# Summing neighbouring exponentials on GpSimd in layer 0's attention, ahead of the matmuls with ones

## The reference

```
scores = einsum('bhqd,bhkd->bhqk', Q, K) + mask      # causal, 1024 x 1024
attn = softmax(scores, axis=-1)
o = einsum('bhqk,bhkd->bhqd', attn, V)
return x + gelu(o) @ Wf + bf
```

## Time and profile before

| | |
|---|---|
| median of 3 runs | 2742.35 us (2739.61 to 2743.72) |
| profiled execution, its own time | 2725.8 us |
| its span | 2723.9 us |
| mean granted TensorE clock | 0.826 of 2.4 GHz |
| busy: TensorE, VectorE, ScalarE, GpSimd | 2218.2, 1513.9, 1402.7, 692.7 us |
| layer 0's attention, from its first matmul with ones to its last | 119 to 288, 779 to 941, 1429 to 1597, 2084 to 2252 us |

### The profile page before, as it was taken

One profiled execution on the slowest core, in us unless ns is written; L12 is line 12 of the kernel. 1 busy time (PEld: TensorE's weight loads), 2 busy tenths in 40 slices (PEclk: granted clock), 3 DMA queues, 4 the chain that ended last, 5 costly groups with the idle time before them and its releaser, 6 DMA issues. The chain is left out here.

```text
span 2723.9 us, 30057 instructions
## 1 busy us (share of the span) xinstructions
PE 2218.2 (81%) x10649; PEld 843.0 (31%) x10649; DVE 1513.9 (56%) x3298; ACT 1402.7 (51%) x2019; POOL 692.7 (25%) x717
## 2 busy tenths in 40 slices
PE   3799867778999886678998987767899998676789
PEld 1223332223433242222443233122343224222244
DVE  2554356666565255675655625577655544566642
ACT  1145437894234533898324453589522454378932
POOL 1012212332422211233331121133242121123324
PEclk9599876568999986676899988567799998666789
DMA  5200131001500023100430003210051002300012
GB/s 137 60 19 2 56 94 38 18 1 40 149 28 19 1 78 94 34 1 1 122 89 24 2 28 95 57 27 1 12 153 44 19 1 78 78 32 18 1 43 89
DMA packets 67845, 128.31 MB, mean 47 GB/s; under 512 B 11396, under 2 KB 24836, under 8 KB 63076
## 3 DMA queue, kind: packets, MB, share of 16 engines
q1 hardware_dynamic: 67696, 126.40, 17.0%
HBM read 109.99 MB, written 15.20 MB: 46 GB/s over the span
## 5 line engine op out<-in xcount | busy, mean ns | idle before, releaser
L1289 DVE TENSOR_REDUCE mx<-ps 128x1 f32<-128x512 f32 (+3 forms) x1248 | 640.0, 553 | 471.3 <-PE ps L655 360.3
L1057 ACT ACTIVATE pr<-ps 128x1024 f32<-128x1024 f32 (+3 forms) x672 | 516.3, 805 | 447.1 <-PE ps L725 444.5
L652 PE MATMUL ps<-kop,qop 72*128 72x512 bf16 (+6 forms) x1248 | 446.2, 380 | 146.0 <-DVE mx L1289 109.0
L725 PE MATMUL ps<-qop,kop 75*128 75x512 bf16 (+7 forms) x1344 | 416.0, 376 | 92.4 <-DVE wb L1349 34.7
L771 PE MATMUL ps<-pr,vt 128*32 128x512 f32 (+3 forms) x2688 | 355.2, 607 | 7.3 <-POOL pr L1576 6.3
L1576 POOL TENSOR_SCALAR_AFFINE_SELECT pr<-pr 128x512 f32<-128x512 f32 x224 | 150.3, 671 | 802.0 <-ACT pr L1057 800.9
L1114 ACT ACTIVATE pr<-ps 128x512 f32<-128x512 f32 x224 | 133.8, 598 | 344.0 <-PE ps L878 280.3
L652 PEld LDWEIGHTS ps<-kop,qop 72*128 72x128 bf16 (+1 forms) x1248 | 123.8, 102 | 544.6 <-DVE mx L1289 335.4
L725 PEld LDWEIGHTS ps<-qop,kop 75*128 75x128 bf16 (+1 forms) x1344 | 122.6, 105 | 325.3 <-ACT pr L1057 133.2
L888 PE MATMUL ps<-pr,w_down 128*128 128x512 f32 x384 | 197.8, 600 | 3.2 <-POOL pr L1567 3.2
L655 PE MATMUL ps<-maskqk,identb 128*128 128x128 bf16 x832 | 199.5, 247 | 0.0
(11 more groups left out here) (309 smaller groups left out, 2989.6 us busy)
## 6 DMA issues: line engine op xcount, KB each, us to landing
wb<-gates_scratch SPq DMA_DIRECT2D x192, 256.0 KB, 3.3
kop<-kparts_scratch SPq DMA_DIRECT2D x32, 576.0 KB
qop<-qparts_scratch SPq DMA_DIRECT2D x96, 192.0 KB
on<-hmax_scratch SPq DMA_DIRECT2D x8, 1024.0 KB, 5.3
kparts_scratch<-on SPq DMA_DIRECT2D x12, 256.0 KB, 2.9
qparts_scratch<-on SPq DMA_DIRECT2D x12, 256.0 KB, 4.5
qparts_scratch<-wb SPq DMA_DIRECT2D x12, 256.0 KB, 2.9
kparts_scratch<-wb SPq DMA_DIRECT2D x12, 256.0 KB, 4.5
```

What stands on the lines that cost most here:

```text
L652: mm = pe.matmul(o, qop[0:k, slot(l, u), j, qb * P:(qb + 1) * P], kop[0:k, slot(l, u), j, k0:k0 + wd], start=True, stop=not diag)
L725: mm = pe.matmul(o, kop[0:k, slot(l, u), 2 * pair + j, kb * P:(kb + 1) * P], qop[0:k, slot(l, u), 2 * pair + j, q0:q0 + wd], start=True, s ...
L1057: nc.scalar.activation(pr[:, g % 3, 2 * pair:2 * pair + 2, o0:o0 + wd], ps[:, bank:bank + 2, o0:o0 + wd], ACT.Exp).then_inc(a.exps, 1)
L1289: ins_ = nc.vector.tensor_reduce(mx[:, nth(l, u) % 2, j, qb, col % 2:col % 2 + 1], ps[:, bank, 0:wd], AX.X, ALU.max, negate=True)
```

## The change

Only layer 0 is touched. Full steps (s = 4 to 7) no longer run the quad with ones. GpSimd adds the exponentials of steps 4 and 5, then those of 6 and 7 (four heads by 512 columns each), into one buffer `pair_sum`, and TensorE runs one quad with ones over each sum: the first behind the value quad of step 7, the second behind step 9. A sum may be overwritten once its quad is done (`pair_used`). The exponentials of layer 0 get a fourth buffer, so that an exponential waits for the step four before it, and in addition for the sum that reads that buffer. The wait for the read-out of bank 5, which stood at step 4, moves to the first quad over a sum.

```diff
+def summed(s):
+    return 4 <= s < 8
+def pairs_until(g):
+    u, s = divmod(g, NS)
+    return 2 * u + (s - 4) // 2 + 1
...
+        depth = (4, 3)
+        def exp_slot(l, g):
+            return pr[:, g % 3] if l else (pr[:, 0], pr[:, 1], pr[:, 2], wb[:, 0])[g % 4]
+        pair_sum = wb[:, 1]
...
                         else:
                             pe.wait_ge(a.o_out, out_before(u, c))
-                            if l == 0:
-                                pe.wait_ge(a.s_out, NC * u + c)
+                            if l == 0 and c == 0:
+                                pe.wait_ge(a.s_out, NC * u)
...
-                        if l and j == 3:
+                        if j == 3 and (l or summed(s)):
                             mm.then_inc(a.pv, 1)
-                    if l == 0:
+                    if l == 0 and not summed(s):
...
+                    if l == 0 and s in (7, 9):
+                        pe.wait_ge(pair_ready, 2 * u + (s == 9) + 1)
+                        if s == 7:
+                            pe.wait_ge(a.s_out, NC * u + 1)
+                        for j in range(4):
+                            mm = pe.matmul(ps[32 * j:32 * j + 32, 5, :], ones32[:], pair_sum[:, j, :],
+                                           start=s == 7, stop=False, tile_position=(0, 32 * j))
+                        mm.then_inc(pair_used, 1)
...
-                        if g >= 3:
-                            act.wait_ge(a.pv, g - 2)
-                        nc.scalar.activation(pr[:, g % 3, 2 * pair:2 * pair + 2, o0:o0 + wd],
+                        if g >= depth[l]:
+                            act.wait_ge(a.pv, g - depth[l] + 1)
+                            if l == 0 and summed((g - depth[l]) % NS):
+                                act.wait_ge(pair_ready, pairs_until(g - depth[l]))
+                        nc.scalar.activation(exp_slot(l, g)[:, 2 * pair:2 * pair + 2, o0:o0 + wd],
...
             for g in range(UNITS * NS):
                 cut(0, g)
+                if g % NS in (5, 7):
+                    pool.wait_ge(at[0].exps, 2 * (g + 1))
+                    if pairs_until(g) > 1:
+                        pool.wait_ge(pair_used, pairs_until(g) - 1)
+                    nc.gpsimd.tensor_tensor(pair_sum, exp_slot(0, g - 1), exp_slot(0, g), ALU.add).then_inc(pair_ready, 1)
                 if g % NS == 4:
                     scale_out(g // NS, 0)
```

More of the change, by code:

```diff
@@ L511, in adaln_kernel @@
         v_ones, tables = sem("v_ones"), sem("tables")
+        pair_ready, pair_used = sem("pair_ready"), sem("pair_used")
         gb_in = [sem(f"gb_in{r}") for r in range(4)]
@@ L771, in values @@
                         mm = pe.matmul(ps[32 * j:32 * j + 32, 4, o0:o0 + wd], vt[:, kb, 32 * h:32 * h + 32],
-                                       pr[:, g % 3, j, o0:o0 + wd], start=kb == 0, stop=last,
+                                       exp_slot(l, g)[:, j, o0:o0 + wd], start=kb == 0, stop=last,
                                        tile_position=(0, 32 * j))
-                        if l and j == 3:
+                        if j == 3 and (l or summed(s)):
                             mm.then_inc(a.pv, 1)
-                    if l == 0:
+                    if l == 0 and not summed(s):
                         for j in range(4):
                             mm = pe.matmul(ps[32 * j:32 * j + 32, 5, o0:o0 + wd], ones32[:],
-                                           pr[:, g % 3, j, o0:o0 + wd], start=kb == 0, stop=last,
+                                           exp_slot(l, g)[:, j, o0:o0 + wd], start=s == 0, stop=last,
                                            tile_position=(0, 32 * j))
                         mm.then_inc(a.pv, 1)
+                    if l == 0 and s in (7, 9):
[6 more added lines that the diff above has]
+                        mm.then_inc(pair_used, 1)
                 def hyp_values(k):
@@ L1573, in cut @@
                 if diag:
-                    past = pr[:, g % 3, :, q0 - c * CH:q0 - c * CH + P]
+                    past = exp_slot(l, g)[:, :, q0 - c * CH:q0 - c * CH + P]
                     pool.wait_ge(at[l].exps, 2 * (g + 1))
```

## The result

Slower. The median of four runs is 2789.52 us (2776.95 to 2795.03) against 2740.98 us (2738.44 to 2743.72) for the kernel before, a ratio of 1.017 [1.0134, 1.0207]. The forecast was 2774 us, in a range of 2748 to 2808. The loss is 48.5 us where 32 were predicted. The profiled execution after took 2776.95 us (span 2775.2), the shortest of its four.

The account below looks back on a forecast made before the run. TensorE, busy 2218 of 2724 us with its full clock granted only part of the time, was taken as the bound. The terms -4.8 + 15.8 + 20.8 gave +32 us on 2742.35, so 2774 us, range 2748 to 2808.

Parts of the forecast that it names:

- The removed quads: Steps 4, 5 and 6 of units with pieces: each loses one quad, 3 x 0.88 = 2.64 us gained.
- The length of the addition: GpSimd addition of 2048 columns: 4.5 us, from the line through its product at 512 and 1024 columns.
- the upper end of 8.0: Longest addition considered, in us: four times the slowest GpSimd group of that size, 1.99 us in layer 1.
- The second addition and the cut behind it: GpSimd before step 8: addition waits for step 7's quads, then the cut; step 8's values at 904.5, 2.0 us lost again.
- units with pieces: Layer 0, 12 units of 44.8 us with VectorE busy 26.4: -0.4 us each before the clock.
- Step 9 and the DMA: End of units with pieces: second sum's quad adds 0.88 us; waits of 0.19 and 0.41 us for the maxima go.
- the term of -4.8 us: Units with pieces, clock left out: -0.4 us per unit, times 12.
- Units without pieces: Each batch's last unit, 4 in all, 26.0 us: +3.9 us each from the late second addition, +15.8 us in sum.
- The clock behind the stall: TensorE's quads behind the stall before step 8 run at half clock: 1.3 us in each of 16 units, +20.8 us.
- The fourth buffer: Layer 0's exponentials: values of three steps before were done anyway, by TensorE's order, so 0.
- the thinner steps: Steps 4 to 6: fall to half clock more often, but have one quad less to run slowly; taken to cancel.

Follow-up runs that it names:

- second profile: Both kernels run again unchanged, each with a new profile: 2739.49 us for the kernel before, 2780.25 us for the changed kernel.
- experiment 2: Changed kernel with a buffer of its own for the second sum, added in two instructions of 1024 columns: 2732.90 us, 0.9964 of the kernel before.
- experiment 4: Changed kernel adding only heads 0 and 1, whose sums stand in for heads 2 and 3: 2733.41 us, 0.9965 of the kernel before.
- experiment 5: Changed kernel with GpSimd's cut of step 8 put ahead of the second addition: 2736.17 us, 0.9997 of the kernel before.
- experiment 6: Changed kernel with the first sum's quad at step 6 in place of step 7: 2741.42 us, 1.0019 of the kernel before.
- Experiment 3: Changed kernel with filler matmuls on TensorE in the stall ahead of step 8's values: 2769.18 us, 1.0089 of the kernel before.
- experiment 7: Kernel before with only the fourth buffer for layer 0's exponentials, no sums: 2737.43 us, 1.0007 of the kernel before.
- experiment 10: Changed kernel without additions or quads over sums, full steps left out of the softmax's sums (measurement only): 2690.52 us, 0.9816 of the kernel before.
- experiment 8: Experiment 2 with the sums only in units with pieces, unit 3 as in the kernel before: 2711.40 us, 0.9882 of the kernel before.
- experiment 9: Experiment 8 with four small zero-weight matmuls ahead of each piece between values of steps 0 and 1: 2736.52 us, 0.9983 of the kernel before.

## Why the prediction was right, and what was mis-sized

The direction and the mechanism were right, and 2789.5 lies in the range. Point by point:

- *The removed quads* ("a quad less shortens such a step by its full 0.88 us"): 0.86 us in each of steps 4, 5 and 6. Right.
- *The length of the addition*, 4.5 us, which no row had: 4.50 and 4.52. Right; the upper end of 8.0 fell. The slow group of the earlier trace rows said nothing of this stage; the stage's own product at 1.283 us did. The GPSIMD Engine Reference of the Trainium skill (section 3.1, Elementwise) has 4497 ns for it, and the trace agrees with 4499.
- *The second addition and the cut behind it*: steps 7 to 8 take 7.26 us, forecast 7.22 (904.5 - 897.28). Right. (From the quad's end to the addition's start it is 0.18 us, 916.84 to 917.02, where the sum had 0.07.) Experiments 2, 4, 5 and 6 each take one link of that chain away (the buffer, the length, the order, the time of the quad), and each time the 5.24 us, or the same sum over two steps, are back in units with pieces.
- *Step 9 and the DMA*: +0.86 for the quad, and steps 10 to 11 go from 2.47 to 1.97 us. Right in kind, but the term of -4.8 us was too small. It took the 0.41 us of one unit for all twelve; four others waited 0.95 to 1.78. The twelve waits for the maxima's DMA were 9.0 us in all (second profile 9.6), and 0.7 (1.0) after, so 8.3 and 8.6 us were gained.
- *Units without pieces*: +3.9 us forecast without the clock (four of them are 15.6, where the sum has 15.8). Measured 30.94 against 25.29, +5.65, of which steps 8 to 9 (4.05 against 2.40) are the clock's: +4.0 without them.
- *The clock behind the stall*, 16 x 1.3 = 20.8 us. Steps 8 to 9 take 4.18 us in the mean with pieces (2.81 at full clock) and 4.13 without (2.40): 12 x 1.37 + 4 x 1.73, with 1.0 more in steps 9 to 10 of two units, make 24.4. Experiment 3 shows it to be the clock. It was between the cases that the trace had shown, and came out at the upper of them: nearly always one step's quads in full. The page TensorE: Matmul & The Clock Gate of the Trainium skill (The HAM clock gate) has an idle array fall to 1.2 GHz; here it fell behind an idle time of 1.95 us, with the clock at 0.53 in the window behind it.
- *The fourth buffer* at 0: 1.0007 in experiment 7. Right.

Two profiles of each kernel give this account, in us (each after against the before beside it):

```
                                         forecast  1st pair   2nd pair
12 units with pieces, layer 0              +10.8     +10.8      +15.3
4 units without pieces, layer 0            +21.0     +23.0      +21.9
layer 1's attention (no edit there)          0       +13.4       +3.4
everything else                              0        +4.0       +8.2
profiled execution                         +32       +51.2      +48.8
```

**The step that failed** is the one on the thinner steps: "I let these cancel". In the first profile of the kernel before six of the steps 5 to 6 and 6 to 7 are slow, in five units, 9.7 us in all with a little of steps 4 to 5; in the second four are, 6.6 us. After, none is. In their place the beginnings of units are slow: steps 1 to 2 over 3.7 us in 6 of 8 units 1 and 2 (7 in the second profile), where it was 1. Over all twelve units steps 0 to 3 take 8.3 us more in the first pair and 12.9 in the second. So it did nearly cancel in the first pair, but not because thin steps "have one quad less to run slowly", and that was luck; experiment 10 shows that those steps don't get slow more often for being thin. Of the 12.9 us, 5.2 are one unit, the first of batch 3; it begins just as slowly in experiment 7, which has the work of the kernel before, so it takes no change for that.

**What was mis-sized** is mainly the rest of the kernel, for which the sum had no term. Layer 0's attention accounts for 33.7 and 37.2 us, against 31.8 forecast; within it, in the first pair, the gain at the DMA was put too small by 3.5 us and the clock's price by 3.6, and the two cancel. 12 to 18 us lie outside it, where both kernels issue the same instructions. Of these, the 13.4 in layer 1 are an accident of the first profile of the kernel before: its four attentions took 1136.3 us there, but 1143.2 to 1152.3 in each of the twelve other profiles, of kernels from 0.98 to 1.017 alike. That accident doesn't explain the miss, though: the second pair ran within 0.5 us of the medians of the result, and has 37.2 us in layer 0's attention, 3.4 in layer 1's and 8.2 elsewhere. The last two, 11.6 us, aren't traced to a cause. Everything outside layer 0's attention took 2062.9 and 2074.5 us in the two profiles of the kernel before, 2071.1 in experiment 7, 2080.5 and 2086.9 after the change, and 2086.2 in experiment 4, which is faster than the kernel before. So the scatter between profiles is as large as what is to be explained; whether the change adds to it stays open.

## What to carry to other kernels

Before work is moved to a slower engine, look at what is queued behind it there, in order, and who waits for that: 4.5 us on an engine that was three quarters idle cost 48 us in all, and putting a 0.64 us instruction ahead of it gave the loss back. A sum that is to be overlapped needs a buffer of its own as well as an idle engine, and here it paid to leave it out where the steps are shorter than it is (experiment 8: both, 0.988). And price a stall of TensorE with the quads behind it at half clock: here 2 us of stall cost 3.4.

## What the runs showed of the hardware

- A GpSimd addition of float32 takes 2.34 us for 1024 columns and 4.50 to 4.52 for 2048, as its product does for 512 and 1024: a line with no step, and no difference whether VectorE is busy beside it with reductions that read PSUM (unit 2) or idle (unit 3), 4.50 and 4.49 us.
- An idle time of 1.95 us between two matmuls was followed by a step at half clock as surely as one of 4.56 us: in the profile after, every one of the 16 stalls was, with 0.50 to 0.58 granted in the 3.4 us behind it. Two to five matmuls whose result nobody reads, in the idle time, kept the clock up in 13 units of 16.
- Where the clock falls in stretches of small matmuls differs between kernels and between executions. The same instructions of steps 1 to 2 were slow in 1 unit of 8 (before, both profiles, and experiment 10) or 3 (experiment 7), in 4 to 8 of 8 in all kernels with additions but experiment 9 (8 in experiment 2), and in 0 of 8 with the fillers of experiment 9 in place. A difference of 1.5 us in one such step need not be an effect of an edit near it; only sums over all units, or the same step slow or fast throughout, could be read.
